# Causal attention regrouped: four units of four heads a batch, scores in two row halves, values as weights in four column quarters

## The reference

```
q = (x @ Wq).reshape(B, T, H, D).transpose(0, 2, 1, 3)      # k, v alike
wei = jnp.einsum('bhtd,bhsd->bhts', q, k) * scale
wei = wei + bias[None]                                      # slope of the head * (s - t)
wei = jnp.where(causal[None, None], wei, -jnp.inf)
wei = jax.nn.softmax(wei, axis=-1)
out = jnp.einsum('bhts,bhsd->bhtd', wei, v)
out = out.transpose(0, 2, 1, 3).reshape(B, T, H * D)
return out @ Wo + bo
```

## Time and profile before

| | us |
|---|---|
| median of 3 runs (562.21, 562.22, 565.05) | 562.22 |
| the profiled execution | 569.07 |
| its span, first to last instruction | 567.2 |
| first bias product to the last batch added | 124.60 |
| six batches in the steady part (309.41 to 400.37) | 90.96 |
| PE, DVE, ACT busy in these | 90.56, 57.00, 42.22 |

### The profile page before, as it was taken

How to read it: one execution, slowest core, us unless ns; L and a number is a source line. 1 busy time by engine, 2 the same in 40 slices (tenths; PEclk the granted TensorE clock), 3 DMA queues, 4 the chain that set the end, 5 groups by cost and what they waited for, 6 DMA issues and landing times.

```text
span 567.2 us, 10216 instructions
## 1 busy us (share of the span) xinstructions
PE 419.8 (74%) x4178; PEld 279.9 (49%) x4178; DVE 271.9 (48%) x669; ACT 159.6 (28%) x333; POOL 93.7 (17%) x106
## 2 busy tenths in 40 slices
PE   9754968796687774568899999999783379988200
PEld 5733737374254442346357777777632253477200
DVE  1355484642425445565546666666436630077122
ACT  2223436262122222302234544444300000144000
POOL 3202020000201112111400000000020077000375
PEclk9567878778769998555789999999986658999655
DMA  8360000000530000000560000000010000132111
GB/s 330 162 245 2 3 2 5 2 18 3 138 77 1 2 1 0 1 0 28 181 293 1 3 5 5 5 5 5 5 31 1 1 25 25 43 102 92 38 41 34
DMA packets 19735, 27.83 MB, mean 49 GB/s; under 512 B 12680, under 2 KB 17416, under 8 KB 19048
## 3 DMA queue, kind: packets, MB, share of 16 engines
q1 hardware_dynamic: 16144, 23.86, 12.2%
q0 software_dynamic: 1536, 1.58, 1.1%
q10 hardware_dynamic: 2016, 1.84, 1.0%
HBM read 21.50 MB, written 6.03 MB: 49 GB/s over the span
## 4 chain that ended last, share of the span: by engine, by line
PE 59%; DVE 21%; ACT 6%; POOL 5%; issue 4%; DMA 3%; DVEq 1%; POOLq 0%; SPq 0%; ACTq 0%
PE bank L1163 49%; PE bank L1166 10%; POOL windows L504 4%; DVE q_sum L784 3%; DVE windows L1134 1%; POOL rstd L451 1%; DVE xT L882 1%; ACT xT L614 1%; DMA hL<-tokens_in 1%; DVEq L1131 1%; ACT xT L726 1%; DVE xT L899 1%; DVE sc_sb L807 1%; DVE sc_sb L811 1%; DVE head_buf L791 1%
## 5 line engine op out<-in xcount | busy, mean ns | idle before, releaser
L1163 PE MATMUL bank<-windows 65*64 65x64 f32 (+3 forms) x976 | 94.0, 263 | 2.3 <-DVE windows L1134 1.9
L1163 PE MATMUL bank<-zero 128*64 128x512 f32 x130 | 71.8, 707 | 2.5 <-DVE hL L1119 1.1
L1163 PEld LDWEIGHTS bank<-windows 65*64 65x64 f32 (+3 forms) x976 | 65.2, 150 | 4.6 <-ACT windows L722 3.1
L451 POOL TENSOR_TENSOR rstd<-ln_v,mhalf 128x6 f32<-128x6 f32 x16 | 21.1, 1326 | 173.6 <-DVE ln_v L877 173.6
L1032 DVE TENSOR_REDUCE xT<-bank 96x2 f32<-96x384 f32 (+1 forms) x48 | 26.5, 552 | 45.4 <-PE bank L1163 45.4
L689 ACT ACTIVATE head_buf<-head_buf 96x384 f32<-96x384 f32 x48 | 25.1, 523 | 66.5 <-DVE head_buf L1035 66.5
L1163 PEld LDWEIGHTS bank<-zero 128*64 128x64 f32 x130 | 19.7, 161 | 48.0 <-issue 45.6
L1166 PE MATMUL bank<-w_tok,xT 128*128 128x128 f32 (+2 forms) x104 | 18.9, 319 | 32.0 <-DVE xT L882 20.0
L1166 PEld LDWEIGHTS bank<-w_tok,xT 128*128 128x128 f32 (+2 forms) x104 | 12.9, 152 | 45.9 <-DVE xT L882 27.5
L1163 PE MATMUL bank<-xT 64*64 64x64 f32 (+2 forms) x192 | 31.6, 310 | 1.5 <-issue 0.7
L504 POOL DMA_INDIRECT windows<-y_slots,addr x24 | 22.8, 948 | 56.2 <-SPq L420 49.2
(11 more groups left out here) (212 smaller groups left out, 635.2 us busy)
## 6 DMA issues: line engine op xcount, KB each, us to landing
big<-in_x SPq DMA_DIRECT2D x4, 2048.0 KB, 11.6
big<-in_w_experts SPq DMA_DIRECT2D x1, 6144.0 KB, 18.1
x_slots<-zero SPq DMA_DIRECT2D x1, 1792.0 KB, 10.8
windows<-x_slots SPq DMA_DIRECT2D x14, 128.0 KB, 2.1
y_slots<-windows ACTq DMA_DIRECT2D x14, 128.0 KB, 1.7
w_ssm<-in_w_ssm SPq DMA_DIRECT2D x1, 448.0 KB, 8.6
hL<-tokens_in SPq DMA_DIRECT2D x2, 192.0 KB, 2.3
tokens_in<-hL SPq DMA_DIRECT2D x2, 192.0 KB, 1.8
```

The source lines that it names most:

```text
L451: pool.tensor_tensor(stat(rstd, k), stat(ln_v, k), mhalf[:, 0:L], ALU.pow).then_inc(s["ln_rstd"], 1)
L1163: return nc.tensor.matmul(out, lhsT, rhs, start=start, stop=stop, **kw)
```

## The change

Units now hold four heads always: even units 96 queries x 96 keys x 4 heads (384 columns), odd units 96 queries x 192 keys x 4 heads (768 columns, two banks). Four units a batch, 32 in all.

- Scores: a product contracts 64 partitions, which hold two heads, of which one is zeroed by a scale of 0 or 1 (`parity`, summed once from the identity). Heads 0 and 1 of a group lie in partitions 0 to 63, heads 2 and 3 in 64 to 127, each half with its own product into its own bank. K is written by ACT alone, in two scaled copies; DVE's part of it and POOL's zeroing of KT go.
- Values: V (96 x 32) is the weight matrix and the transposed weights (96 columns) stream, four heads into four partition quarters of bank 1. The sums come from the same stream with a 96 x 32 block of ones as weights. The result has features on partitions, so the four transposes of o_n and their copy go.
- DVE divides a whole group of four heads for 192 queries at once: a reciprocal of 128 x 192 sums and a product of the same size, twice a batch.
- The steps are set further apart: PE turns unit n-2 and multiplies unit n-3 in round n (before n-1 and n-2). The projections of the next batch come behind the values product, with waits for Q_ready, K_ready, V_ready and, for Q from batch 2 on, h3_ready of the batch two before.

The core of the diff (removed lines of the old loops and definitions are in the code above and left out):

```diff
-UNITS = 6 * B
+UNITS = 4 * B
...
+        QT = over(4, [128, 2, 2, T])
+        KT = over(3, [128, 2, 2, 2, T])
+        parity = sb("parity", [128, 2])
+        V = over(4, [HALF, 2, 2, 2, 4 * AD])
+        ones = over(4, [HALF, AD])
+        S = [over(5, [HALF, 2, 4, HALF]), over(5, [HALF, 2, 4, T])]
+        S_max = over(1, [HALF, 4, 2, 2])
+        PT = over(3, [HALF, 6, 4, HALF])
+        o_inv = over(4, [128, T])
+        oT = over(4, [128, 2, 2, T])
...
-        def unit_shape(n):
-            return (4, HALF) if n % 3 == 0 else (2, T)
+        def keys_of(n):
+            return T if n % 2 else HALF
+        def scores_of(n):
+            at = 6 if n % 2 else 4
+            return banks[0:HALF, at:at + 2, 0:2 * keys_of(n)].rearrange("p a (h k) -> p a h k", h=2)
         def unit_of(n):
-            slot = n % 6
-            return 4 * (slot // 3) + (0, 0, 2)[slot % 3], int(slot % 3 > 0)
+            return S[n % 2][:, (n // 2) % 2, :, :]
         def qkv_bank(b, which):
-            return bank[0] if b else bank[(3, 4, 0)[which]]
+            return bank[0] if b else bank[(6, 7, 0)[which]]
+        def chunks_to(n):
+            return 3 * (n // 2) + (3 if n % 2 else 1)
+        def chunk_range(n):
+            return range(chunks_to(n) - (n % 2) - 1, chunks_to(n))
...
-            pool.memset(KT[:, :, :, :, :], 0.0).then_inc(s["ones_set"], 1)
-            pool.memset(V[:, :, :, :, AD:AD + 1], 1.0).then_inc(s["ones_set"], 1)
+            pool.memset(ones[:, :], 1.0).then_inc(s["ones_set"], 1)
...
             def key(b):
                 act.wait_ge(s["QKV_ps"], 3 * b + 2)
-                for k in (2, 3):
-                    q = slice(AD * k, AD * k + AD)
-                    ins = copy(KT[q, b % 2, :, k, :], qkv_bank(b, 1)[q, 0:2 * T].rearrange("p (m t) -> p m t", m=2))
+                for k in range(2):
+                    ins = nc.scalar.activation(KT[:, b % 2, :, k, :], qkv_bank(b, 1)[:, 0:2 * T].rearrange("p (g t) -> p g t", g=2),
+                                               ACT.Copy, scale=parity[:, k:k + 1])
                 ins.then_inc(s["K_ready"], 1)
...
+            for n in range(UNITS + 1):
+                b, slot = divmod(n, 4)
                 if n < UNITS:
                     act.wait_ge(s["S_centered"], n + 1)
...
+                    nc.scalar.activation(unit_of(n), unit_of(n), ACT.Exp).then_inc(s["S_exped"], 1)
+                if n == 0 or slot == 3 and b + 2 < B:
+                    query(b + 2 if n else 1)
+                if slot == 0 and b + 1 < B:
                     key(b + 1)
...
+                if n:
+                    m = n - 1
+                    if m >= 4:
+                        act.wait_ge(s["PV_ps"], m - 3)
+                    for c in chunk_range(m):
+                        act.wait_ge(s["PT_ps"], c + 1)
+                        copy(PT[:, c % 6, :, :].rearrange("p h q -> p (h q)"), bank[2 + c % 2][0:HALF, 0:UNIT]).then_inc(s["PT_ready"], 1)
...
+            red(parity[:, :], ident.rearrange("p (a k d) -> p k a d", a=2, k=2), AX.XY, ALU.add)
...
+            def center(n):
+                dve.wait_ge(s["S_ps"], n + 1)
+                link(red(S_max[:, n % 4, :, :], scores_of(n), AX.X, ALU.max))
+                if n >= 4:
+                    dve.wait_ge(s["PT_ps"], chunks_to(n - 4))
+                tt(unit_of(n).rearrange("p (a h) k -> p a h k", a=2), scores_of(n),
+                   S_max[:, n % 4, :, :].unsqueeze(3).broadcast_to([HALF, 2, 2, keys_of(n)]), ALU.subtract).then_inc(s["S_centered"], 1)
+            def divide(i):
+                dve.wait_ge(s["PV_ps"], 2 * i + 2)
+                if i >= 4:
+                    dve.wait_ge(s["wo_ps"], i // 2 - 1)
+                link(nc.vector.reciprocal(o_inv[:, :], bank[1][:, AT_SUM:AT_SUM + T]))
+                tt(oT[:, (i // 2) % 2, i % 2, :], bank[1][:, 0:T], o_inv[:, :], ALU.mult).then_inc(s["o_ready"], 1)
+            def add_attention(b):
+                dve.wait_ge(s["wo_ps"], b + 1)
+                dve.wait_ge(s["hb_ready"], 1 + b // 4)
+                h = hN[:, 2 * b:2 * b + 2, :]
+                tt(h, bank[0][0:HALF, 0:2 * D].rearrange("p (a h) -> p a h", a=2), h, ALU.add).then_inc(s["h3_ready"], 1)
...
+            for n in range(UNITS + 4):
+                b, slot = divmod(n, 4)
                 if n < UNITS:
...
+                    center(n)
+                if n % 2 and 3 <= n < UNITS + 2:
+                    divide((n - 3) // 2)
+                if slot == 2 and b + 1 < B:
                     value(b + 1)
...
+                if slot == 3 and b:
+                    add_attention(b - 1)
...
+            def unit_scores(n):
+                b, g = n // 4, (n // 2) % 2
+                keys, first = keys_of(n), HALF * (n % 2)
+                if n >= 2:
+                    pe.wait_ge(s["S_centered"], n - 1)
+                for a in range(2):
+                    mm(scores_of(n)[:, a, :, :], identb[:, :], alibi[:, 4 * g + 2 * a:4 * g + 2 * a + 2, T - keys:T], start=True, stop=False,
+                       skip_group_check=True)
+                for a in range(2):
+                    q = slice(2 * AD * a, 2 * AD * a + 2 * AD)
+                    ins = mm(scores_of(n)[:, a, :, :], QT[q, b % 2, g, first:first + HALF], KT[q, b % 2, g, :, 0:keys],
+                             start=False, stop=True, skip_group_check=True)
+                ins.then_inc(s["S_ps"], 1)
+            def turn_unit(n):
+                pe.wait_ge(s["S_exped"], n + 1)
+                for k, c in enumerate(chunk_range(n)):
+                    if c >= 2:
+                        pe.wait_ge(s["PT_ready"], c - 1)
+                    for j in range(4):
+                        ins = transpose(bank[2 + c % 2][0:HALF, HALF * j:HALF * j + HALF],
+                                        unit_of(n)[:, j, HALF * k:HALF * k + HALF], HALF)
+                    ins.then_inc(s["PT_ps"], 1)
+            def weighted_values(n):
+                b, g = n // 4, (n // 2) % 2
+                pe.wait_ge(s["PT_ready"], chunks_to(n))
+                if n % 2 == 0 and n:
+                    pe.wait_ge(s["o_ready"], n // 2)
+                first = HALF * (n % 2)
+                parts = chunk_range(n)
+                for at in (0, AT_SUM):
+                    for k, c in enumerate(parts):
+                        for j in range(4):
+                            q = slice(AD * j, AD * j + AD)
+                            ins = mm(bank[1][q, at + first:at + first + HALF], ones[:, :] if at else V[:, b % 2, k, g, q],
+                                     PT[:, c % 6, j, :], start=k == 0, stop=k == len(parts) - 1, skip_group_check=True)
+                ins.then_inc(s["PV_ps"], 1)
+            def attention_out(b):
+                pe.wait_ge(s["o_ready"], 2 * b + 2)
+                pe.wait_ge(s["V_ready"], min(b + 3, B))
+                for a in range(2):
+                    for g in range(2):
+                        ins = mm(bank[0][0:HALF, D * a:D * a + D], oT[:, b % 2, g, HALF * a:HALF * a + HALF],
+                                 we("Wo")[:, D * g:D * g + D], start=g == 0, stop=g == 1)
+                ins.then_inc(s["wo_ps"], 1)
...
+            for n in range(UNITS + 4):
+                b, slot = divmod(n, 4)
                 if n < UNITS:
...
+                    if slot == 0 and b:
+                        pe.wait_ge(s["Q_ready"], b + 1)
+                        pe.wait_ge(s["K_ready"], b + 1)
+                    unit_scores(n)
+                if 2 <= n < UNITS + 2:
+                    turn_unit(n - 2)
+                if 3 <= n < UNITS + 3:
+                    weighted_values(n - 3)
+                if slot == 0 and b + 1 < B:
+                    pe.wait_ge(s["V_ready"], b + 1)
+                    if b >= 2:
                         pe.wait_ge(s["h3_ready"], b - 1)
...
+                    qk(b + 1, 0)
+                if slot == 1 and b + 1 < B:
+                    pe.wait_ge(s["Q_ready"], b + 2)
+                    qk(b + 1, 1)
+                if slot == 2 and b + 1 < B:
+                    pe.wait_ge(s["K_ready"], b + 2)
                     value(b + 1)
...
+                if slot == 3 and b:
+                    attention_out(b - 1)
```

More of the change, by code:

```diff
@@ L102, in packed @@
             return t, (lambda key: t[:, at[key][0]:at[key][0] + at[key][1]])
-        bank = [ctx.enter_context(nc.psum_tensor(f"bank{i}", [128, 512], F32)) for i in range(8)]
+        banks = ctx.enter_context(nc.psum_tensor("bank", [128, 8, 512], F32))
+        bank = [banks[:, i, :] for i in range(8)]
         img_tok = nc.dram_tensor("tokens_in", (B, T, D), F32, kind="Internal").ap()
@@ L681, in key @@
                 ins.then_inc(s["K_ready"], 1)
             query(0)
-            act.wait_ge(s["ones_set"], 2)
             key(0)
-            for n in range(UNITS + 4):
-                b, slot = divmod(n, 6)
+            for n in range(UNITS + 1):
+                b, slot = divmod(n, 4)
                 if n < UNITS:
```

(33 more changed lines are left out.)

118 lines of the change are left out of this document (10 added, 108 removed).

## The result

| | before | changed |
|---|---|---|
| median, runs on one chip | 563.63 (4 runs) | 610.70 (605.21 to 616.67, 4 runs) |
| the profiled execution, its span | 569.07, 567.2 | 605.21, 603.4 |
| first bias product to the last batch added | 124.60 | 166.68 |
| before that, behind it, of the span | 288.10, 154.50 | 284.45, 152.27 |

The changed kernel takes 1.078 times as long (95% interval 1.066 to 1.0905). Forecast were 620, its own range 602 to 634, and 627 for an execution like the profiled one. The loop is 42.1 us longer; the 5.9 us that the stretches around it are shorter lie in code that the change leaves alone, apart from POOL's smaller memsets.

What follows compares the result with a forecast made beforehand. PE's stream was taken to bound the loop, 15.16 us a batch. Half clock adds 58 to 68, less 4.4 saved; taking +58, 562.2 + 58 = 620 us, its own range 602 to 634, overall 557 to 634.

Steps and rivals of the forecast that it cites:

- the sum of the blocks: PE's steady batch at full clock: blocks of 11.0 us and 19 drains of 0.09 make 12.7 us.
- the scores' overlap: PE's score products: the two row halves run beside each other, 1.96 us less a batch.
- a change of shape: Changing the shape in which PE's array is used: 0.16 us each, 13 more a batch, +2.1 us.
- the first sum: PE's batch from 15.16 us, less scores, values and transposes, plus shape changes: 12.9 us.
- Values: PE's values passes in four column quarters run beside each other: 2.1 us less a batch.
- The two waits: PE each batch: 2.3 us for h3_ready behind DVE's division, about 0.9 behind ACT's copies of K.
- 4.4 were reckoned: Whole attention loop if the clock stays full: 120.2 us against 124.6, so -4.4 us.
- The clock: TensorE's clock in the loop falls at the first 2.3 us wait, in batch 2: +58 us; chance 0.44.
- the short wait: PE's transposes of the next unit wait about 0.9 us each batch behind ACT's copies of K.
- the few rows of the new products: Loop's 96-row and 64-row products, unlike full-row ones, do not bring the clock back; ffn's 64-row products stay at half.
- stays down to the end of the loop: After batch 2 the clock stays at half: 25.8 to 27.5 us a batch, 10.1 to 11.7 more than warm.
- The second rival: Clock falls at the loop's waits and climbs back within some microseconds: 561 to 575 us; chance 0.22.

Runs made afterwards that it cites:

- experiment 8: Fastest version (DVE's add ahead of the division, ACT's K copies late) with both score products of a unit on rows 0 to 63: 557.9 us, 14.52 a batch.
- experiment 10: Fastest version (add ahead of the division, K's copies late) with both units of a group in one PE round: 553.1 us, ratio 0.982.
- experiment 1: `add_first`: changed kernel with DVE adding the batch before ahead of dividing the group of heads: 550.6 us, ratio 0.978.
- experiment 4: Changed kernel with DVE's add ahead of the division and ACT's K copies behind those of the transposed weights: 544.4 us, ratio 0.968; again 541.2, ratio 0.960.
- experiment 7: Changed kernel with the reciprocal taken of 8 of the 192 sums per partition: 582.0 us, ratio 1.028.
- experiment 3: Kernel before the change with a PE wait of about 2.2 us added in each of batches 2 to 6: 619.5 us, ratio 1.101.
- experiment 5: `key_late`: changed kernel with ACT's K copies behind those of the transposed weights, the long wait kept: 591.1 us.
- experiment 2: `warm_in_wait`: changed kernel with two 128-row products on zeros issued by PE in its long wait: 579.1 us, ratio 1.020.
- experiment 6: Changed kernel with 128-row products on zeros in the long wait and ACT's K copies behind those of the weights: 553.3 us, ratio 0.981.

## Why the prediction was right, step by step

- **Durations.** The reciprocal of 128 x 192 was put at 1.35 us:

```profile
L1036 DVE RECIPROCAL windows<-bank 128x192 f32<-128x192 f32 x16 | 21.7, 1358 | 62.0 <-PE bank L1171 62.0
```

  It came out at 1.358. The estimate of 1.6 from the Trainium skill ("VectorE: DVE Perf Modes", the fixed hardware budget) is too high; the slope of the earlier trace rows carried further.
- **PE's stream.** 12.7 was the sum of the blocks, 12.68 is the batch when nothing waits; that close, it is in part luck, since single terms missed by 0.1 and more. Of its terms the scores' overlap was 1.96 and measured 1.84 (experiment 8), a change of shape 0.16 in the first sum, 0.09 and its load in the second, and measured 0.09 in all (experiment 10, whose expectation has 0.13). Values last 0.80 and 0.47 a unit, 2.54 a batch with 4 drains, against 2.1 + 0.36.
- **The two waits.** 2.3 and 0.9 were forecast, 2.16 and 0.80 measured. Experiment 1 less experiment 4 is 0.84 a batch for the second. As an estimate, the warm batch of the changed kernel is then 13.52 + 2.16 = 15.68 (15.8 forecast); experiment 7 agrees, with 14.49 at full clock (309.77 to 324.26) for a wait of 1.01. The loop without the falls in its batches would be 110.3 (experiment 1, first bias to last add) + 5 x 2.16 = 121.1. The forecast's 120.2 is a slip: its terms add up to 8.8 + 13.7 + 5 x 15.8 + 19.1 = 120.6. Without those falls the change would have saved 3.5 us, where 4.4 were reckoned.
- **The clock.** That it would fall at the first of these waits, in batch 2, and not before, is what 308.90 to 315.70 shows, and experiments 1, 3 and 5 make the wait the cause of this first fall. The falls that followed came behind the short wait, which the forecast took to be harmless to the clock; experiments 2, 5 and 6 show that it is not beside another wait. Of the forecast's reasons, one stands (the fall after 1.32 us of waiting in the earlier trace rows) and one does not: the forecast leaned on the few rows of the new products for the clock staying down. The old loop's full-row scores stayed down just as well in experiment 3.
- **The size.** The step that was mis-sized is "stays down to the end of the loop": 25.8 to 27.5 a batch, against 23.85. The granted clock was full for 3.4 us of each. Over the loop the clock cost 166.68 - 121.1 = 46 us where the middle of the range had 62. The forecast for the median was 9 us high, but for the profiled execution, 605.21 against 627, it was 22 high: that execution was the shortest of the four and had the highest mean clock (0.731, the others 0.707 to 0.726). So the median lies closer to the forecast than the trace does.
- **The second rival** (falls and climbs back soon) is what the Trainium skill ("TensorE: Matmul & The Clock Gate", HAM oscillation) describes, there for waits for DMA; the trace agrees in so far as each batch had its rise, but the rise came 4.7 us behind the first long wait and 5.9 to 6.0 behind the others, and held for 3.4 us. In experiment 2 it came within 0.5 us of the end of the full-row zeros.
- **What stays open:** why the clock came back for 3.4 us a batch in the changed kernel and for 6.8 to 13.7 in `key_late`, and why the short wait was harmless in all batches of `add_first` and not in two of `warm_in_wait`. The instructions right around the short wait are the same in both; what differs is what lies between two of them: in `warm_in_wait` the zeros and a wait of 0.2 us, in a batch of 15.66 us (354.87 to 370.53) where `add_first` has 13.52. Nor is it known what in PE's work brings the clock back: in experiment 3 it stayed down with PE busy all but two waits. No run here varied one of these alone, and each kernel was traced once or twice.

## What to carry to other kernels

A change that makes PE's stream shorter can put an engine's queue order in front of PE that did not matter before: read, for each semaphore that PE waits for, what stands ahead of the signal in the other engine's queue, and what its new length is. On a PE-bound stretch a wait is priced not by its own length (here 11 us in all) but by the clock that it takes with it (46). When a wait can't be moved away, fill it with full-row products, but take the short waits beside it away too: of the 57 us between the means of the changed kernel (608.9) and of the version with both (552.1), filling alone left 21 and moving the short wait alone 32.

## What was not expected of the hardware

- The clock fell within 0.8 us of the end of a wait of 0.80 us in three kernels: in five batches of the changed kernel, and in some batches only where the wait 5 to 6 us ahead of it was filled (experiment 2) or 1.01 us long (experiment 7). Without such a neighbour it left the clock full (experiment 1).
- Half clock can hold while PE is nearly always busy: 71.03 of 75.10 us in the old loop with added waits, of which two waits of 2.04 are the rest, with scores over 128 rows.
- Weight passes into the same 32 columns cost 0.058 us each in a row of eight (1.85 / 32), against 0.025 in alternating quarters (0.80 / 32), and in a row of four next to nothing more (0.49 against 0.47 for 16).
